# Hybrid sequence model: the channel value product as three fp32r products one period later, its low part on GpSimd

## What is computed

```python
xn = layer_norm(x, ln1_w, ln1_b);  lx = time_shift(xn)
k, v, r = (mixed with time_mix_k, _v, _r) @ w_key, w_value, w_recept
# wkv, a recurrence over the tokens of a sequence, per channel:
#   tau2 = max(eps - w, k); d1 = exp(eps - w - tau2); d2 = exp(k - tau2)
#   alpha = d1*alpha + d2*v ; beta = d1*beta + d2
#   out = (e1*alpha + e2*v) / (e1*beta + e2)
x = x + wkv(...) * sigmoid(r) @ w_output
xn2 = layer_norm(x, ln2_w, ln2_b);  lx2 = time_shift(xn2)
fk = (xn2*f_time_mix_k + lx2*(1 - f_time_mix_k)) @ f_w_key       # 256 -> 1024
fr = (xn2*f_time_mix_r + lx2*(1 - f_time_mix_r)) @ f_w_recept    # 256 -> 256
vk = square(relu(fk)) @ f_w_value                                # 1024 -> 256
x = x + sigmoid(fr) * vk
```

## Time and profile before

| | |
|---|---|
| time of the runs | 1428.28 us median of 3 (1426.02 to 1428.88) |
| profiled execution, span | 1423.3 us, first to last instruction |
| mean granted TensorE clock | 0.968 |
| TensorE, VectorE, ScalarE, GpSimd busy | 94%, 64%, 48%, 44% of the span |
| mix stage | about 615 to 1060 us of the span |

### The profile page before, as it was taken

One profiled execution on the slowest core, in us unless ns is written; L12 is line 12 of the kernel. 1 busy time (PEld: TensorE's weight loads), 2 busy tenths in 40 slices (PEclk: granted clock), 3 DMA queues, 4 the chain that ended last, 5 costly groups with the idle time before them and its releaser, 6 DMA issues. The chain is left out here.

```text
span 1423.3 us, 28011 instructions
## 1 busy us (share of the span) xinstructions
PE 1341.5 (94%) x7638; PEld 1132.6 (80%) x7639; DVE 905.0 (64%) x2171; ACT 683.0 (48%) x1541; POOL 629.5 (44%) x583
## 2 busy tenths in 40 slices
PE   6999997799999999966899999998979999999997
PEld 4999986688888888834777777777868888888886
DVE  5877888454444444457888898887864454444443
ACT  4576765233333333354687669766643333333332
POOL 4768663355555555424132222222213555555553
PEclk9999997999999999998999999999989999999999
DMA  8575853566665333370000000000326766633333
GB/s 274 209 266 196 296 206 134 167 161 163 167 158 116 52 54 58 45 225 0 1 16 31 0 30 30 30 0 31 120 89 176 169 158 161 167 71 58 54 52 42
DMA packets 100874, 157.86 MB, mean 111 GB/s; under 512 B 10256, under 2 KB 60688, under 8 KB 100816
## 3 DMA queue, kind: packets, MB, share of 16 engines
q1 hardware_dynamic: 73120, 118.67, 24.5%
q0 software_dynamic: 27264, 37.82, 16.6%
q10 hardware_dynamic: 432, 0.66, 0.1%
HBM read 95.89 MB, written 61.21 MB: 110 GB/s over the span
## 5 line engine op out<-in xcount | busy, mean ns | idle before, releaser
L1367 POOL DMA_INDIRECT out_x<-second_y,second_add_token x71 | 112.7, 1587 | 154.0 <-DMA out_x<-second_y,second_add_token 71.4
L1367 POOL DMA_INDIRECT x_rows<-first_y,first_add_token x70 | 111.3, 1590 | 150.4 <-ACT first_y L1405 88.8
L1358 POOL DMA_INDIRECT xs<-normed_rows,gather_token x140 | 140.5, 1004 | 45.9 <-issue 41.5
L1475 DVE TENSOR_TENSOR first_hT_lo<-bank,first_hT_hi 128x512 fp32r<-128x512 f32 x71 | 49.1, 692 | 159.9 <-ACT first_hT_hi L1395 159.9
L1475 DVE TENSOR_TENSOR second_hT_lo<-bank,second_hT_hi 128x512 fp32r<-128x512 f32 x71 | 49.1, 692 | 158.1 <-ACT second_hT_hi L1395 155.8
L166 PE MATMUL bank<-ring,first_xT_hi 128*128 x284 | 118.9, 418 | 3.4 <-DVE first_xT_lo L1463 3.4
L166 PE MATMUL bank<-ring,second_xT_hi 128*128 x284 | 118.9, 419 | 2.2 <-DVE second_xT_lo L1463 2.2
L168 PE MATMUL bank<-ring,first_xT_lo 128*128 x284 | 112.9, 398 | 0.0
L168 PE MATMUL bank<-ring,second_xT_lo 128*128 x284 | 112.8, 397 | 0.0
L167 PE MATMUL bank<-ring,first_xT_hi 128*128 x284 | 112.6, 397 | 0.0
L167 PE MATMUL bank<-ring,second_xT_hi 128*128 x284 | 112.4, 396 | 0.0
(11 more groups left out here) (455 smaller groups left out, 3909.0 us busy)
## 6 DMA issues: line engine op xcount, KB each, us to landing
ring<-split_weights SPq DMA_DIRECT2D x192, 256.0 KB, 3.1
a_wraw<-in_L_ffn_w SPq DMA_DIRECT2D x21, 512.0 KB, 6.3
split_weights<-a_whi SPq DMA_DIRECT2D x21, 512.0 KB, 2.6
split_weights<-a_wlo SPq DMA_DIRECT2D x21, 512.0 KB, 3.5
normed_rows<-xg SPq DMA_DIRECT2D x16, 528.0 KB, 3.1
x_rows<-x SPq DMA_DIRECT2D x8, 512.0 KB, 7.2
x<-x_rows SPq DMA_DIRECT2D x8, 512.0 KB, 6.0
out_x<-x SPq DMA_DIRECT2D x8, 512.0 KB, 3.2
```

The lines of the kernel that those rows point to most:

```text
L1358: nc.gpsimd.indirect_dma_start(xs[q][:], None, normed_dram[:], bass.IndirectOffsetOnAxis(ap=gather_token[q][:], axis=0)).then_inc(loaded[q ...
L1367: nc.gpsimd.indirect_dma_start(x_dram[:], bass.IndirectOffsetOnAxis(ap=add_token[q][:], axis=0), y[q], None, compute_op=ALU.add).then_inc( ...
L1475: nc.vector.tensor_tensor(hT_lo[par][:].rearrange("p k t -> p (k t)"), th_bank[par][:], hT_hi[par][:].rearrange("p k t -> p (k t)").bitcas ...
```

## The change

In the channel part `hT` is kept twice: ScalarE writes the relu to `hT_raw` and its square, rounded to fp32r, to `hT_hi`. GpSimd squares `hT_raw` in place, two chunks (128x1024) at a time, and subtracts `hT_hi` from it, which gives `hT_lo` (`low_hidden`). The weight `f_w_value` is split into `fv_hi` (ScalarE) and `fv_lo` (GpSimd, 128x2048) once before the loop. The value product is `hT_hi` by `fv_hi`, `hT_hi` by `fv_lo` (`value_hi`) and `hT_lo` by `fv_hi` (`value_lo`), all fp32r, and both its halves stand in the next period behind the transposes of `xn2`; in the last period both batches' products are there. `project_r` is cut in two halves around the transposes. GpSimd's program has four `low_hidden` per period (the pair of chunks 6 and 7 in the next one), both `add_channel` in the next period, and no wait for `num_ready` ahead of `add_mixed`, which stands behind the first `rstd`. On VectorE `mix_channel` and `low_key` stand ahead of `softmax_end`, both `finish` are in the next period, and `dv` stands behind the scans of `be`. On ScalarE `row_exp` moves behind `gaps_of_step`, and `evacuate_xn2` ahead of it. `dv`, `num`, `den`, `al` and `gT` have no buffers of their own: they lie in `k`, `v`, `rho`, `eps` and `v`.

```diff
-        over = overlaid(nc, [(f"b_over{i}", [P, KC * N], F32R) for i in range(13)])
-        flat = {n: sb(n, [P, KC * N])[:] for n in ("xk", "xv", "xr", "k", "v", "sg", "d1", "d2", "dv", "num", "rho", "den", "gT", "dT")}
-        flat.update({n: sb(n, [P, KC * (N + 1)])[:] for n in ("xnT", "eps", "al", "be")})
+        hT_lo, fv_lo, xfk_lo, *over = overlaid(nc, [("b_hT_lo", [P, FCH, N], F32R), ("b_fv_lo", [P, FCH, C], F32R),
+                                                    ("b_xfk_lo", [P, KC, N], F32R)]
+                                               + [(f"b_over{i}", [P, KC * N], F32R) for i in range(9)])
+        hT_raw, fv_raw, xfk = sb("hT_raw", [P, FCH, N]), sb("fv_raw", [P, FCH, C]), sb("xfk", [P, KC, N])
+        flat = {n: sb(n, [P, KC * N])[:] for n in ("xk", "xv", "xr", "k", "v", "sg", "d1", "d2", "rho", "dT", "be")}
+        flat.update({n: sb(n, [P, KC * (N + 1)])[:] for n in ("xnT", "eps")})
+        hT_hi, fv_hi = sb("hT_hi", [P, FCH, N], F32R), sb("fv_hi", [P, FCH, C], F32R)
         wk_s, wv_s, wr_s, wo_s, wf_s = (sb(f"w{n}", [P, KC, C]) for n in "kvrof")
-        fv_s = sb("fv", [P, FCH, C])
         fk_hi, fk_lo = sb("fk_hi", [P, KC, F], F32R), sb("fk_lo", [P, KC, F], F32R)
...
-        den, rho, d1, d2, dT = (Shelf(flat[n]).take([P, KC, N]) for n in ("den", "rho", "d1", "d2", "dT"))
-        dv, num, gT = (Shelf(flat[n]).take([P, KC, N]) for n in ("dv", "num", "gT"))
-        xnT, eps, al, be = (Shelf(flat[n]).take([P, KC, N + 1]) for n in ("xnT", "eps", "al", "be"))
-        xb, xn2, xn2T = sb("xb", [P, TB, C]), xn, sb("xn2T", [P, KC, N + 1])
-        xfk, xfr = sb("xfk", [P, KC, N]), sb("xfr", [P, KC, N])
-        xfk_hi, xfk_lo = sb("xfk_hi", [P, KC, N], F32R), sb("xfk_lo", [P, KC, N], F32R)
-        hT, fs = sb("hT", [P, FCH, N]), sb("fs", [P, 2, N])
-
-        fk_raw = hT[:, 0:KC * F // N, :].rearrange("p (k a) n -> p k (a n)", k=KC)
+        rho, d1, d2, dT, be = (Shelf(flat[n]).take([P, KC, N]) for n in ("rho", "d1", "d2", "dT", "be"))
+        xnT, eps = (Shelf(flat[n]).take([P, KC, N + 1]) for n in ("xnT", "eps"))
+        dv, num, den, al = k, v, rho, eps[:, :, 1:N + 1]
+        gT = num
+        xn2T_flat = sb("xn2T", [P, KC * (N + 1)])
+        xb, xn2, xn2T = sb("xb", [P, TB, C]), xn, Shelf(xn2T_flat[:]).take([P, KC, N + 1])
+        xfr, xfk_hi, fs = sb("xfr", [P, KC, N]), sb("xfk_hi", [P, KC, N], F32R), sb("fs", [P, 2, N])
+
+        fk_raw = hT_raw[:, 0:KC * F // N, :].rearrange("p (k a) n -> p k (a n)", k=KC)
...
-                    nc.scalar.activation(hT[:, m, :], xb_[m % 4][:], ACT.Relu).then_inc(h_relu, 1)
+                    nc.scalar.activation(hT_raw[:, m, :], xb_[m % 4][:], ACT.Relu).then_inc(h_relu, 1)
                     act.wait_ge(h_relu, FCH * b + m + 1)
-                    nc.scalar.activation(hT[:, m, :], hT[:, m, :], ACT.Square).then_inc(h_ready, 1)
+                    nc.scalar.activation(hT_hi[:, m, :], hT_raw[:, m, :], ACT.Square).then_inc(h_ready, 1)
...
-            nc.scalar.activation(fv_s[:], fv_s[:], ACT.Copy, scale=0.5).then_inc(halved, 1)
+            nc.scalar.activation(fv_raw[:], fv_raw[:], ACT.Copy, scale=0.5).then_inc(halved, 1)
+            act.wait_ge(halved, 2)
+            nc.scalar.activation(fv_hi[:], fv_raw[:], ACT.Copy).then_inc(fv_hi_ready, 1)
...
             def period(b):
                 if has_before(b, 2):
                 if has_next(b, 1):
                     evacuate_k(b + 1)
                 norm2(b)
+                if has_next(b, 1):
+                    evacuate_v(b + 1)
+                evacuate_xn2(b)
+                if has_next(b, 1):
+                    gaps_of_step(b + 1)
                 if has_before(b, 2):
                     row_exp(b - 2)
-                if has_next(b, 1):
-                    evacuate_v(b + 1)
-                if static(b, 0):
-                    evacuate_xn2(b)
-                if has_next(b, 1):
-                    gaps_of_step(b + 1)
-                if not static(b, 0):
-                    evacuate_xn2(b)
                 if has_next(b, 1):
                     weights_of_step(b + 1)
                     evacuate_r(b + 1)
...
+            def low_hidden(b, m):
+
+
+                wait_apart(pool, h_ready, FCH * b + m + 2, passed["pool"])
+                raw = hT_raw[:, m:m + 2, :]
+                nc.gpsimd.tensor_tensor(raw, raw, raw, ALU.mult).then_inc(squared, 1)
+                wait_apart(pool, squared, (FCH * b + m + 2) // 2 if isinstance(b, int) else FCH // 2 * b + m // 2 + 1, passed["pool"])
+                nc.gpsimd.tensor_tensor(hT_lo[:, m:m + 2, :], raw, hT_hi[:, m:m + 2, :].bitcast(F32), ALU.subtract).then_inc(h_lo_ready, 1)
+
+            pool.wait_ge(fv_hi_ready, 1)
+            nc.gpsimd.tensor_tensor(fv_lo[:], fv_raw[:], fv_hi[:].bitcast(F32), ALU.subtract).then_inc(fv_lo_ready, 1)
+
             def period(b):
                 rstd(mv2, shift2, own_2, var2_ready, rstd2_ready, b)
+                if has_before(b, 1):
+                    low_hidden(b - 1, FCH - 2)
+                add_mixed(b)
                 if has_next(b, 2):
                     rstd_in(b + 2)
                 if has_before(b, 1):
+                    add_channel(b - 1, 0)
                     add_channel(b - 1, 1)
+                low_hidden(b, 0)
+                if has_before(b, 1):
                     rstd(mvg, shiftg, own_c, varg_ready, rstdg_ready, b - 1)
-                if has_next(b, 1):
-                    wait_apart(pool, num_ready, b + 2, passed["pool"])
-                add_mixed(b)
-                add_channel(b, 0)
+                for m in range(2, FCH - 2, 2):
+                    low_hidden(b, m)
 
             over_periods(pool, period)
+            low_hidden(B - 1, FCH - 2)
+            add_channel(B - 1, 0)
...
-            def decayed_value(b):
+            def denominator(b):
 
                 r_.round(b)
+                dve.wait_ge(expd, 6 * b + 4)
+                for i in range(KC):
+                    last = nc.vector.tensor_tensor_scan(be[:, i, :], d1[:, i, :], d2[:, i, :], 0.0, ALU.mult, ALU.add)
+                r_.link(last)
                 dve.wait_ge(kvr_evac, 6 * b + 4)
-                dve.wait_ge(expd, 6 * b + 3)
                 r_.link(nc.vector.tensor_tensor(dv[:], d2[:], v[:], ALU.mult))
-                dve.wait_ge(expd, 6 * b + 4)
-
-            def denominator(b):
+
+            def numerator(b):
 
                 for i in range(KC):
-                    last = nc.vector.tensor_tensor_scan(be[:, i, 1:N + 1], d1[:, i, :], d2[:, i, :], 0.0, ALU.mult, ALU.add)
+                    last = nc.vector.tensor_tensor_scan(al[:, i, :], d1[:, i, :], dv[:, i, :], 0.0, ALU.mult, ALU.add)
+                r_.link(last)
                 dve.wait_ge(expd, 6 * b + 6)
-                nc.vector.tensor_tensor(num[:], rho[:], v[:], ALU.mult)
-                r_.link(last)
-                nc.vector.tensor_tensor(den[:], rho[:], be[:, :, 0:N], ALU.add)
-
-            def numerator(b):
-
-                for i in range(KC):
-                    last = nc.vector.tensor_tensor_scan(al[:, i, 1:N + 1], d1[:, i, :], dv[:, i, :], 0.0, ALU.mult, ALU.add)
-                r_.link(last)
-                r_.link(nc.vector.tensor_tensor(num[:], num[:], al[:, :, 0:N], ALU.add))
+                r_.link(nc.vector.tensor_tensor(num[:], rho[:], v[:], ALU.mult))
+                nc.vector.tensor_tensor(den[:, :, 1:N], rho[:, :, 1:N], be[:, :, 0:N - 1], ALU.add)
+                r_.link(nc.vector.tensor_tensor(num[:, :, 1:N], num[:, :, 1:N], al[:, :, 0:N - 1], ALU.add))
 
...
+                mix_channel(b)
+                low_key(b)
                 if has_before(b, 2):
                     softmax_end(b - 2)
                 if static(b, B - 1):
                     dve.wait_ge(top_taken, B - 2)
                     early_choices(nc, placing, route, idx, const)
-                mix_channel(b)
-                low_key(b)
                 if has_before(b, 1):
+                    finish(b - 1, 0)
                     finish(b - 1, 1)
-                if has_next(b, 1):
-                    decayed_value(b + 1)
                 if has_next(b, 1):
                     denominator(b + 1)
                     numerator(b + 1)
...
-                finish(b, 0)
 
             over_periods(dve, period)
+            finish(B - 1, 0)
             for n in range(4, EARLY):
...
-            def value_tile(out, src, j):
+            def value_hi(b, h):
+
+
+                if has_next(b, 2):
+                    pe.wait_ge(kvr_evac, 6 * b + 15 + h)
+                pe.wait_ge(h_relu, FCH * b + FCH)
+                pe.wait_ge(h_ready, FCH * b + FCH)
+                for j in range(2):
+                    for i in range(FCH):
+                        out, part = xb_[2 + h][:, j * C:(j + 1) * C], hT_hi[:, i, (2 * h + j) * P:(2 * h + j + 1) * P]
+                        nc.tensor.matmul(out, part, fv_hi[:, i, :], start=(i == j == 0), stop=False, skip_group_check=True)
```

(48 more changed lines are left out.)

43 lines of the change are left out of this document (24 added, 19 removed).

## The result

The changed kernel takes 1520.25 us, median of four runs (1519.24 to 1521.33); the kernel before took 1428.58 beside it (four runs, 1426.02 to 1430.49). The ratio is 1.0647, interval [1.0632, 1.0662]: 92 us slower. Forecast were 1527.0 (1475 to 1572), slower with a chance of 0.95. The sum is right within 7 us, but its parts are not: the periods cost 18 us less than forecast, the end of the stage 16 us more. The experiments say why, and part of the agreement is luck.

The account below looks back on a forecast made before the run. TensorE was taken to set the pace now, VectorE's chain with GpSimd's turns after the change. Periods +81.1, before them +9.1, after them +9 gave 99 us: 1522.5 of span, 1527 as a time, range 1475 to 1572.

Parts of the forecast that it names:

- The turns: VectorE instructions with two SBUF inputs and GpSimd instructions reading SBUF exclude each other for whole instructions, in strict alternation.
- Ahead of the first gT: Period 0 and before: `fv_lo` +4.4 us; TensorE waits for `gT` until 709.3 instead of 700.2, +9.1 (3 to 14).
- TensorE's gain: Value product of two halves falls from 13.8 to 11.3 us per batch: 2.5 us, if TensorE stays the bound.
- The signs: Per period: GpSimd 31 us busy or more, VectorE 55 to 60, TensorE waiting 10 or more for `gT`, clock below 1.
- The blocked time: VectorE blocked by GpSimd's turns in a steady period: 4.7 + 7.1 + 2.0 + 4.7 = 18.5 us.
- "No wait" for the value product: At VectorE's two finishes (to 36.2 us) TensorE's values are done at 32, so nothing is waited for.
- rival 1: Turns cost little, but `finish(b-1, 1)` waits for the value product until 27.8 us; period 50 to 51, 1454 us; chance 0.06.
- The clock: TensorE's standing halves its clock, output product takes 6.9 us; 0 to 2 us per period, 0 taken.
- 2.4 for luck: One of six blocked low operations taken off a steady period, for those falling on work without turns: 63.9 to 61.5 us.
- rival 4: Half of the turns: VectorE's unlinked pairs keep GpSimd out; 56 us per period, 1492 us; chance 0.12.
- Behind the last gT: Period 7: two batches' value products (22.5 us for 20.7) and six low operations in turns; together +9 (2 to 15).

Follow-up runs that it names:

- the memset run: Changed kernel with each GpSimd squaring and subtraction of the low part replaced by a memset of the same tile; 1475.9 us.
- the run with products that nothing reads: Changed kernel plus unread TensorE products, 24 behind the receptance product and 8 behind the gate transposes; 1514.0 us, ratio 1.061.
- the run where both edits stood: Changed kernel without the low part, second finish behind the `be` scans, unread TensorE products (20 and 8) ahead of the output product; 1460.8 us.

## Why the prediction was right, and where its steps were wrong

**Right.** *The turns.* They are there, whole instructions and one for one, as read from the earlier trace rows: `rho`, `dT`, `gT` and the numerator's and denominator's operations grew, the reciprocal kept 6.55, and the memset run shows that it takes reading. *Ahead of the first gT:* its start moved by 7.7 and its end by 9.5 (it took 2.98), where +9.1 was forecast; `fv_lo` is 4.3 of it, for 4.4 (VectorE's pair at 654.74 takes 6.61 us, before the change 2.31). *TensorE's gain:* half a value product is 5.6 us, and is no use.

**The signs.** GpSimd is busy for 35.2 us of a period (31 or more), the granted clock is 0.91 and 0.85 in the two stretches. But VectorE's busy time is 52.8, under the 55 to 60; of TensorE's 10 us of waiting only 3.04 are for gT; and the scans did not grow (2.32 for the pair of `eps`, 3.38 for `be`). At `eps` it was GpSimd that waited: its squaring takes 2.85 there.

**The blocked time, mis-sized.** I had 18.5 us per period. VectorE's busy time is 52.83 against the 41.73 of the earlier trace rows, 11.1 more, plus the 1.0 it paid already: about 12. Chunks 4, 5 block 3.3 (`gT` +1.2, `dT` +2.1), not 4.7; chunks 6, 7 and the first add 3.9 (`rho` +3.55, `dT` +0.3), not 7.1; chunks in the sums 3.5, not 4.7; the adds at the scans of `be` 1.1, not 2.0. Two things were off: squaring a tile by itself takes 1.89, and I had taken the 2.36 of an addition for all eight; and one of the three operations at `rho` always fell beside the statistics of `begin`, which take no turn.

**"No wait" for the value product: the step that failed.** I had the values done at 32 and the second finish at 34.9. The value product ends 30.8 us after gT (I took 3.6 us for the output product, it took 6.3), VectorE is at the finish earlier since it is blocked less, and it waits 1.95 there. So the period was closed by TensorE and VectorE in series, not by VectorE's chain. The order alone, which my sum priced at nothing and rival 1 at 1454 with a chance of 0.06, brings 1476 to 1478 by itself. Rival 1 was no alternative to the turns; it was there with them, and hidden under them. Its period of 50 to 51 measured 52.80: its finish at 27.8 came at 31.0, the half clock of the output product (2.8) being most of the difference.

The clock is the same step seen from the other side. It was forecast at 0 to 2 us per period and 0 taken, because the output product was needed only at 10.1 and TensorE was said not to be what the period waits for. VectorE did not wait for that product, but everything behind it on TensorE came later, the value product with it: about 1 us of a period in the changed kernel, and the 1.15 us between the two kinds of period without the low part.

As a sum: 42.6 of VectorE, about 12 blocked and 3.8 waited make 58. The working had 42.6, 18.5 and 2.2, with 0.6 for starts, less 2.4 for luck: 61.5. Over the periods +63.4 for +81.1. By its number rival 4, with 56 us per period, is as near as the sum, but not by its reason: the unlinked pair of `rho` did let GpSimd in (4.97 for 1.42).

**Behind the last gT: +24.8 for +9.** This was the other mis-sized term. Without the low part it is still +14.4 (455.8 against 441.4), so the displaced value product brings more than the 1.8 us that I had by adding up TensorE's time. All of it lies within the stage: from the last gT to the stage's last gate product are 79.2 us there (1019.7 to 1098.9), against 64.7 before (981.9 to 1046.6), and 8.5 of the difference are there one gate product earlier (53.0 against 44.6). How it splits between the half clock and the later keys was not tried. The low part brings the other 10.4. GpSimd's timeline in the last period of the changed kernel:

```profile
1098.48 2.81 POOL L1990 TENSOR_TENSOR b_hT_raw<-b_hT_raw 128x1024 f32<-128x1024 f32 x1
...
1113.66 3.10 POOL L1992 TENSOR_TENSOR b_hT_lo<-b_hT_raw,b_hT_hi 128x1024 fp32r<-128x1024 f32 x1 [0.18 <-POOL b_hT_raw L1990]
```

VectorE's, beside it:

```profile
1098.38 1.15 DVE L339 TENSOR_TENSOR b_dT<-b_be,lane 128x960 f32<-128x960 int32 x1
...
1102.29 3.37 DVE L339 TENSOR_TENSOR b_xn2T<-b_be,lane 128x960 f32<-128x960 int32 x1
...
1118.15 0.69 DVE L2169 SCALAR_TENSOR_TENSOR b_fs<-b_fs,bank 128x512 f32<-128x512 f32 x1 [3.59 <-PE bank L2357]
```

The last six low operations take turns with VectorE's two-input work for 18.3 us (1098.48 to 1116.76), where they need 12.8 alone (three of 1.89, three of 2.37). The high part's products cover them until 1109.8; from there TensorE waits 0.93 and 5.32 us for the last two pairs, VectorE's operations are 2.9 to 3.4 us instead of 1.15 to 1.22, and it waits 3.59 for TensorE. I had the turns, and let the products cover nearly all of them. The two errors are -18 and +16, so the total is right by luck: it looks better than the working was.

## What to carry to other kernels

Before a wait or a blocked stretch is added to the sum, find the closed loop that sets the period and ask which part of it the stretch lies in: blocked time cost nothing ahead of a wait (2 us at `rho` and the `dT` behind it) and nearly its full length behind it (1.0 of 1.2 at `gT`). And look at single periods beside the mean: where an operation's length varies within a run, the periods say whether it is on the loop. A product that "only moves" into the stretch between one engine's result and the other engine's first use puts most of its length into the period (4.7 us here for half a value product of 5.6), though its engine had room for it. And work for GpSimd that reads SBUF needs a place beside instructions that take no turns, instruction by instruction, not a share of free time.

## What was not expected of the hardware

- GpSimd's product of a tile with itself, 128x1024 in place, takes 1.89 us undisturbed; the difference of two tiles of that shape 2.37.
- GpSimd's memset of 128x1024 takes 0.95 us, and 64 of them left VectorE's busy time within 1.2 us of 918.5.
- GpSimd and VectorE alternate one instruction for one also over a long stretch: from 1098.48 to 1116.76 six of GpSimd's took 2.8 to 3.2 us each and VectorE's beside them 2.9 to 3.4.
- TensorE's output product took 6.33 us behind idle stretches of 6.91 and 3.04 us; in the run with products that nothing reads 5.40 behind 1.71 and 2.08, and 3.72 behind 1.99 and 0.49; and 3.62 in the run where both edits stood and no such gap came ahead of it.
